# Layer 0's rotary q and k from even and odd columns: two products a row for four, six packing transfers for three

## What is computed

```python
def _rope(x):
    ...
    xr = x[..., 0::2]
    xi = x[..., 1::2]
    o = jnp.stack([xr * cos - xi * sin, xr * sin + xi * cos], axis=-1)
    return o.reshape(x.shape)
qkv = x @ W_qkv.T + b_qkv
...
q = _rope(q)
k = _rope(k)
...
scores = jnp.einsum('bhqd,bhkd->bhqk', q, k) / math.sqrt(D)
w = jax.nn.softmax(scores, axis=-1)
out = jnp.einsum('bhqk,bhkd->bhqd', w, v)
```

## Time and profile before

| | |
|---|---|
| median of three runs | 1804.51 us (1802.91 to 1811.77) |
| span of the profiled execution | 1781.4 us |
| outside the span | 23.1 us against the median |
| TensorE busy | 1516.1 us, 85% |
| VectorE busy | 1140.7 us, 64% |
| ScalarE busy | 866.4 us, 49% |
| GpSimd busy | 443.6 us, 25% |
| mean granted clock of TensorE | 0.903 |

### The profile page before, as it was taken

One profiled execution on the slowest core, in us unless ns is written; L12 is line 12 of the kernel. 1 busy time (PEld: TensorE's weight loads), 2 busy tenths in 40 slices (PEclk: granted clock), 3 DMA queues, 4 the chain that ended last, 5 costly groups with the idle time before them and its releaser, 6 DMA issues.

```text
span 1781.4 us, 41543 instructions
## 1 busy us (share of the span) xinstructions
PE 1516.1 (85%) x11849; PEld 962.0 (54%) x11849; DVE 1140.7 (64%) x3250; ACT 866.4 (49%) x1971; POOL 443.6 (25%) x542
## 2 busy tenths in 40 slices
PE   5457999998989769999986688898999698999997
PEld 4123666665655258888875245555554255555554
DVE  6734666666667755656556556566668567777774
ACT  1023444454445324444431255556565177788887
POOL 3475332322322202222223712212213100000000
PEclk9567999998999659999995689999999689999999
DMA  8442454454444113333220324333342011111110
GB/s 257 131 156 65 137 168 145 141 172 124 143 136 136 26 54 137 113 124 142 107 83 26 113 79 131 123 105 121 109 127 76 30 44 51 47 51 49 47 52 11
DMA packets 127956, 182.18 MB, mean 102 GB/s; under 512 B 14824, under 2 KB 107296, under 8 KB 125424
## 3 DMA queue, kind: packets, MB, share of 16 engines
q1 hardware_dynamic: 94944, 141.94, 24.7%
q10 hardware_dynamic: 26112, 25.17, 4.8%
q0 software_dynamic: 6816, 14.02, 2.2%
HBM read 145.84 MB, written 42.84 MB: 106 GB/s over the span
## 4 chain that ended last, share of the span: by engine, by line
PE 62%; DVE 16%; issue 8%; ACT 4%; POOL 4%; DMA 4%; DVEq 1%; SPq 0%; ACTq 0%; POOLq 0%
PE pO L739 8%; PE pH L530 7%; PE pH L622 7%; PE pY L543 6%; PE pT_ L596 6%; PE pY L630 6%; DVE mx L1343 4%; PE pS L682 3%; PE pS L704 3%; POOL sorted_x L995 2%; ACT pex L853 2%; PE pT_ L594 2%; PE pT_ L514 2%; DVE ob L1421 1%; PE pS L506 1%
## 5 line engine op out<-in xcount | busy, mean ns | idle before, releaser
L853 ACT ACTIVATE pex<-pT_ 128x512 f32<-128x512 f32 (+1 forms) x768 | 427.0, 560 | 481.1 <-PE pT_ L596 367.2
L1343 DVE TENSOR_REDUCE mx<-pS 128x2 f32<-128x512 f32 x512 | 346.9, 689 | 137.0 <-PE pS L573 122.5
L596 PE MATMUL pT_<-stk 32*128 32x256 f16 x1024 | 199.0, 283 | 71.5 <-DVE mx L1343 29.3
L894 POOL DMA_INDIRECT home_y<-ysb,home x117 | 115.1, 984 | 547.9 <-DVE ysb L1365 348.4
L573 PE MATMUL pS<-stk 32*128 32x256 f16 x1024 | 207.0, 289 | 22.6 <-DVEq L1086 17.6
L739 PE MATMUL pO<-pex,va 128*9 128x256 f32 (+1 forms) x3072 | 204.7, 387 | 2.7 <-ACT pex L853 2.7
L846 ACT ACTIVATE wb<-pH,b 128x256 f32<-128x256 f32 x256 | 107.3, 470 | 113.3 <-PE pH L530 112.9
L596 PEld LDWEIGHTS pT_<-stk 32*128 32x128 f16 x1024 | 55.0, 93 | 183.8 <-issue 87.6
L530 PE MATMUL pH<-XT,w 128*128 (+1 forms) x512 | 131.9, 385 | 1.1
L622 PE MATMUL pH<-xsT,wb 128*128 128x128 f32 x888 | 132.5, 294 | 0.3 <-ACT xsT L822 0.3
L630 PE MATMUL pY<-wb,hbs 128*128 128x128 f32 x888 | 128.5, 288 | 3.0 <-DVE ysb L1365 3.0
(11 more groups left out here) (222 smaller groups left out, 2626.8 us busy)
## 6 DMA issues: line engine op xcount, KB each, us to landing
wb<-in_w SPq DMA_DIRECT2D x111, 514.0 KB, 4.9
stk<-packed_qk ACTq DMA_DIRECT2D x96, 256.0 KB, 2.7
packed_qk<-qk SPq DMA_DIRECT2D x144, 128.0 KB, 2.1
wb<-gates_turned SPq DMA_DIRECT2D x8, 2048.0 KB, 7.0
pex<-gates_turned SPq DMA_DIRECT2D x8, 2048.0 KB, 7.0
xsb<-sorted_x SPq DMA_DIRECT2D x111, 64.5 KB, 2.1
sorted_x<-in_c_places SPq DMA_DIRECT2D x4, 1548.0 KB, 16.1
XN<-home_y SPq DMA_DIRECT2D x16, 256.0 KB, 5.1
```

Of the source, the lines that this page charges most:

```text
L596: return pe.matmul(bank[:, part * T:(part + 1) * T], key, stk[rows, side, j, 0:T], start=True, stop=True)
L853: ins = act.activation(pex[:, k % 8, 0:n], bank[:, 0:n], ACT.Exp)
L894: pool.indirect_dma_start(YH, bass.IndirectOffsetOnAxis(ap=home[:, place_:place_ + 1], axis=0), ysb[:, place_, :], None).then_inc(sem(f"ho ...
L1343: ins = dve.tensor_reduce(mx[:, :, j, col], bank.rearrange("p (c n) -> p c n", c=2), AX.X, ALU.max)
```

## The change

In layer 0 the weights of P0 are the 64 even columns of q beside the 64 even columns of k, and those of P1 the odd ones; each step makes one product of 256 columns in place of two. VectorE reads the same 256 columns twice, once for the cosine and once for the sine or the negative sine, and writes the four 128 x 256 pieces so that GpSimd's sum holds, in its first 256 columns, the even results and in the next 256 the odd ones, q on partitions 0 to 63 and k on 64 to 127. q and k now lie on different partitions, so a transfer of the packing takes one of them: six transfers of 64 partitions (64 KB each), where there were three of 128 (128 KB each). All bytes of `packed_qk` are as before. The count that its readers wait for is 96 a row instead of 48. Layers 2 and 3 pack as before.

```diff
-        wq0 = sb("wq0", [P, 5, P])
-        bq0 = sb("bq0", [P, 4])
+        wq0 = sb("wq0", [P, 3, P])
+        bq0 = sb("bq0", [P, 2])
-        rope0 = sb("rope0", [P, 4, T])
+        rope0 = sb("rope0", [P, 3, T])
...
+        def packings(l):
+            return 96 if l == 0 else 48
...
                     elif kind == "P":
                         w = {0: wq0, 2: wq2, 3: wq3}[l]
-                        for n, which in enumerate({0: [2 * k, 2 * k + 1]}.get(l, [k])):
-                            ins = pe.matmul(bank[:, n * T:(n + 1) * T], w[:, which, :],
-                                            XT[:, bass.ts(turn.row(2), T)], start=True, stop=True)
-                        ins.then_inc(s("S_full"), 1)
+                        pe.matmul(bank[:, 0:T], w[:, k, :], XT[:, bass.ts(turn.row(2), T)], start=True, stop=True)\
+                          .then_inc(s("S_full"), 1)
...
-                        act.wait_ge(s("packed"), PRIMED + turn.count(48, 144))
+                        act.wait_ge(s("packed"), PRIMED + turn.count(packings(l), 3 * packings(l)))
...
                             for half in range(2):
+                                turned_by = 0 if half == k else 1 + k
                                 ins = dve.scalar_tensor_tensor(
-                                    qkf[:, half, side], bank[:, half * T:(half + 1) * T],
-                                    bq0[:, 2 * k + half:2 * k + half + 1], rope0[:, 2 * k + half, :],
-                                    ALU.add, ALU.mult)
+                                    qkf[:, half ^ k, half * T:(half + 1) * T], bank[:, 0:T], bq0[:, k:k + 1],
+                                    rope0[:, turned_by, :], ALU.add, ALU.mult)
...
+                if turn.layer == 0:
+                    for b, low in enumerate((2, 1)):
+                        to = QK.rearrange("(x i) r (b t) -> b r x i t", i=2, b=2)[b]
+                        for r in range(3):
+                            sp.dma_start(to[r], qk16[b * P // 2:(b + 1) * P // 2, QK_LOW if r == low else QK_HIGH, :])\
+                              .then_inc(s("packed"), 16)
+                    return
                 for r, blocks in enumerate((slice(1, 3), slice(1, 4, 2), slice(0, 3, 2))):
...
-    c["c_rope0"] = np.stack([cs * f(QSCALE), sn * f(QSCALE), cs, sn], axis=1).astype(f)
+    pair, scale = np.arange(P) % (DH // 2), np.where(np.arange(P) < P // 2, f(QSCALE), f(1.0))[:, None]
+    cs, sn = cos[:, pair].T * scale, sin[:, pair].T * scale
+    c["c_rope0"] = np.stack([cs, sn, -sn], axis=1).astype(f)
...
-    o["wq0"] = np.stack([q, q[:, swap], k, k[:, swap], v], axis=1)
+    pairs = [np.concatenate([q[:, even + n], k[:, even + n]], axis=1) for n in range(2)]
+    o["wq0"] = np.stack(pairs + [v], axis=1)
```

More of the change, by code:

```diff
@@ L680, in take_turn @@
                         w = {0: wq0, 2: wq2, 3: wq3}[l]
-                        for n, which in enumerate({0: [2 * k, 2 * k + 1]}.get(l, [k])):
-                            ins = pe.matmul(bank[:, n * T:(n + 1) * T], w[:, which, :],
-                                            XT[:, bass.ts(turn.row(2), T)], start=True, stop=True)
-                        ins.then_inc(s("S_full"), 1)
+                        pe.matmul(bank[:, 0:T], w[:, k, :], XT[:, bass.ts(turn.row(2), T)], start=True, stop=True)\
+                          .then_inc(s("S_full"), 1)
                     elif kind == "V":
                         pe.wait_ge(s("row_staged"), PRIMED + turn.row(2))
-                        w = {0: wq0[:, 4, :], 2: wq2[:, 2, :], 3: wq3[:, 2, :]}[l]
+                        w = {0: wq0[:, 2, :], 2: wq2[:, 2, :], 3: wq3[:, 2, :]}[l]
                         pe.matmul(bank[:, 0:P], xtb[:, nxt, k * P:(k + 1) * P], w, start=True, stop=True)\
@@ L1304, in take_turn @@
                         if turn.n > -2:
-                            dve.wait_ge(s("packed"), PRIMED + turn.count(48, 96))
+                            dve.wait_ge(s("packed"), PRIMED + turn.count(packings(l), 2 * packings(l)))
                         side = slice(k * T, (k + 1) * T)
@@ L1621, in shape_constants @@
     e = np.arange(P) % DH
-    cs = cos[:, e // 2].T
-    sn = (sin[:, e // 2] * np.where(e % 2 == 0, -1.0, 1.0).astype(f)).T
-    c["c_rope0"] = np.stack([cs * f(QSCALE), sn * f(QSCALE), cs, sn], axis=1).astype(f)
+    pair, scale = np.arange(P) % (DH // 2), np.where(np.arange(P) < P // 2, f(QSCALE), f(1.0))[:, None]
+    cs, sn = cos[:, pair].T * scale, sin[:, pair].T * scale
+    c["c_rope0"] = np.stack([cs, sn, -sn], axis=1).astype(f)
     ang2 = np.arange(B, dtype=f)[:, None] * freqs[None, :]
@@ L1636, in lay_out @@
     o = {}
-    swap = np.arange(P) ^ 1
+    even = np.arange(0, P, 2)
     o["x"] = a["L0_attn_x"].reshape(B * T, P)
@@ L1640, in lay_out @@
     q, k, v = wt[:, 0:P], wt[:, P:2 * P], wt[:, 2 * P:]
-    o["wq0"] = np.stack([q, q[:, swap], k, k[:, swap], v], axis=1)
+    pairs = [np.concatenate([q[:, even + n], k[:, even + n]], axis=1) for n in range(2)]
+    o["wq0"] = np.stack(pairs + [v], axis=1)
     bq, bk = a["L0_attn_b_qkv"][0:P], a["L0_attn_b_qkv"][P:2 * P]
-    o["bq0"] = np.stack([bq, bq[swap], bk, bk[swap]], axis=1)
+    o["bq0"] = np.stack([np.concatenate([bq[even + n], bk[even + n]]) for n in range(2)], axis=1)
     o["bv0"] = a["L0_attn_b_qkv"][2 * P:]
```

## The result

The changed kernel took 1863.09 us (median of four, 1860.43 to 1867.01) against 1804.38 us: 1.0316 times the time before, with a 95% interval of 1.0293 to 1.0338. That is 59 us slower where 13 us faster was forecast. The profiled execution has a span of 1862.2 us inside a time of 1864.0.

The account below looks back on a forecast made before the run. TensorE was taken as the bound (62% of the chain), in layer 0 from turn 2 to 13. 1781.4 - 11.9 + 1.3 - 2.4 = 1768.4, with 23.1 outside the span 1791.5 us; range 1784 to 1804.

Parts of the forecast that it names:

- The products: P0 and P1 in layer 0's twelve turns: half the TensorE products go, 11.9 us gained, bounds 7.5 and 12.8.
- Rival 2: VectorE keeps the gain and only P0's 0.53 us a turn passes: 6.2 us gained, 1798 us; chance 0.12.
- The issue pace: Three more packing issues on SyncE at 0.43 us each make the last packing land 1.3 us later, between 0.9 and 2.3.
- The room: Slack before the next turn's first scores: 1.82 us with a 2.7 us spread, hiding the delay in eleven turns; otherwise 0.37.
- SyncE's next loads: Loads behind the packing in SyncE's queue, for a block six blocks ahead: said to have a whole turn.
- Rival 1: Spread lands late every turn, first scores stall 0.93 us: 11.5 us lost in all, 1804 us; chance 0.12.
- Rival 3: Half transfers queue behind one another, first scores stall 1.93 us: 23.5 us lost against 11.9 gained, 1816 us; chance 0.08.
- The rule of the Trainium skill: Transfers to disjoint partition halves serialize; read as a half taking as long as the whole, delay 1.5 us, sum 0.2 less.
- The slow stretches: Stretches at granted clock 0.50 ahead of P0, in seven of twelve turns: two fewer taken, 2.4 us gained.
- Time around the span: Outside the profiled span of 1781.4 us: 23.1 us, up to the three-run median of 1804.5, added to the forecast.

Follow-up runs that it names:

- the products alone: The changed kernel's two products a row with the three packing transfers of the kernel before: 1798.1 us, ratio 0.9947.
- six whole transfers: The kernel before with layer 0 packed by six transfers of 128 partitions and one block of 256 columns each: 1814.5 us, ratio 1.0047.
- the order kept: The changed kernel with SyncE holding back the expert weights until ScalarE has issued the first half of the spread: 1812.2 us, ratio 1.0021.
- the filling run: The changed kernel with eight identity products on TensorE ahead of the wait for the spread at each turn's head: 1830.6 us, ratio 1.0133.
- the first, short execution: The first profiled execution of the unchanged kernel before, on which the prediction rests: span 1781.4 us, against 1802.4 us when profiled again.

## Why the prediction was wrong, step by step

**The products** lay within their bounds of 7.5 and 12.8 us, at the lower end. I had 11.9 us passing; the products alone gave 7.7 us (5.2 to 13.7 by the interval), a figure that includes whatever fewer slow stretches gave. Rival 2, with 7.5 us, fits it as well, and no run separates the two. There are 48 records of them instead of 96, and P0 takes 0.64 us in the chain of the turn shown (0.53 forecast). With the products alone VectorE's wait for them is 25.4 us, 14 times, against 36.7, 24 times; in the changed kernel it is 34.2 us. There nothing of the gain is left: the halves cost the same with the old products (1862.8 us) as with the new ones (1863.1), since the chain hangs on packing and spread.

**The issue pace** is the step that failed first. I multiplied three more issues by the 0.43 us of the earlier trace rows, rows that hold only transfers of 128 partitions. The pace is 0.61 us with 64, and the delay from first issue to spread is 5.28 us against 3.12, 2.2 us more: near my upper bound of 2.3, not the 1.3 that I took. For six whole transfers, where the pace holds, the spread goes 3.99 us after the first issue, 0.9 us more.

**The room** failed next. I took 2.7 us for the spread's landing, and read the 4.15 us of turn 9 as the mark of a late packing alone. The row that would have told is in the trace of before, SyncE's timeline of that turn:

```profile
424.07 0.36 SPq L1476 DMA_DIRECT2D wb<-in_w  x1
```

The weights left 0.14 us ahead of the spread at 424.21; in the ordinary turns before they leave some 1.2 us behind it. In the changed kernel the two leave within 0.2 us of each other, either one first, in nine of the eleven turns that still load weights. So the room wasn't 1.82 us, nor 0.37; it was the margin of these two issues, for with the order kept the same delay of 2.2 us leaves 0.4 us of waiting in all turns together. I had dismissed SyncE's next loads with "have a whole turn": true for their own lateness, but not for what they meet. This meeting I had put at nothing, and its cover was an order of issues that nothing in the code held. Rival 1, at a chance of 0.12, had the late landing in every turn and named the weights; it paired them with the delay of 1.3 us.

**Rival 3**, at a chance of 0.08, had the place right (the wait for the first half of the spread at each head) and the delay (2.3). Its price was short: it counted the stall, 1.93 us a turn (measured 1.7), and not the lower clock behind it, 3 us a turn by the filling run. The rule of the Trainium skill that stood beside it ("DMA: Bandwidth & Descriptors", "Rules for kernel authors") gave the right advice for this case, one transfer of 128 partitions. The mechanism that it names isn't what the trace shows: the engines idle between halves, and the issue is what takes longer. I also read it beyond its words, for it doesn't say that a half takes as long as the whole, and with the wrong sign: 1.5 us in place of 1.3 make the sum 0.2 us more, not less.

**The slow stretches** were taken as two fewer, five of twelve turns. With the products alone the trace holds the lower level ahead of P0 in five; in the changed kernel it is nine, and there is a new one of 6.8 us or more behind each of ten waiting heads. My argument looked only at the idle ahead of P0, not at idle time that the change itself makes.

**Time around the span**: I put 23.1 us outside it. It is 1.8 us (1864.0 against 1862.2; 1804.2 against 1802.4). The 23.1 us were in truth mostly the lead of the first, short execution. In the sum they did no harm, since they only brought it back to the median that it is compared with.

## What to carry to other kernels

A price per transfer holds for its shape: cutting a transfer into halves of the partitions can make each issue dearer than the whole. Where a short transfer ends a loop, look which bulk transfer is issued near it and what holds that order; if it's chance, a wait that keeps it can be worth more than the change at hand. Price a new stall with the clock that follows it: here the lower clock cost nearly twice the stall.

## What the runs showed of the hardware

- An issue on SyncE's queue took 0.43 us for 128 partitions with 64 or 128 KB, and 0.61 us for 64 partitions with 64 KB, contiguous or every second one.
- A spread of 256 KB issued 1.2 us or more ahead of a 514 KB load on another engine's queue landed mostly after 2.6 to 3.3 us; issued within 0.1 us of it or behind it, mostly after 3.8 to 5 us. At 0.16 us ahead it went either way (3.11 and 4.74 us). With a load of 8 KB in the same place it landed after 3 us.
- Transfers whose outermost dimension has 2 entries moved 41 GB/s at a DMA share of 0.14.
- Behind 1.7 us of idle time, TensorE ran 6.9 us at a granted clock of 0.51; with that idle time filled it stayed at 1.00.
